# Small-head attentions: value jobs of a group in two pairs, with the turning of the next maxima behind the second pair

## What is computed

```python
# L2: causal
Q = relu(queries @ Wq + bq); K = relu(keys @ Wk + bk); V = relu(values @ Wv + bv)   # 16 heads, d = 16
scores = where(key_masks == 0, NEG, Q_ @ K_^T / d**0.5); scores = where(tril == 0, NEG, scores)
out = softmax(scores) @ V_;  out = relu(out @ Wo + bo);  x = normalise(queries + out)
# L3: banded self attention, then full cross attention, then the feed-forward part
mask = (j <= i) & (i - j < 64); bias = slopes[:, None, None] * (j - i)
x = layernorm(x + mha(x, x, ..., mask, bias)); x = layernorm(x + mha(x, mem, ..., None, None))
x = layernorm(x + gelu(x @ w1 + b1) @ w2 + b2)
```

## Time and profile before

| what | value |
|---|---|
| median of three runs | 1582.44 us |
| lowest, highest | 1578.88, 1588.16 us |
| the profiled execution, its own time | 1586.47 us |
| its span, first to last instruction | 1584.7 us |
| mean granted TensorE clock | 0.978 |
| TensorE busy | 1434.6 us, 91% of the span |
| VectorE busy | 864.1 us, 55% |
| ScalarE busy | 716.6 us, 45% |

### The profile page before, as it was taken

How to read it: one execution, slowest core, us unless ns; L and a number is a source line. 1 busy time by engine, 2 the same in 40 slices (tenths; PEclk the granted TensorE clock), 3 DMA queues, 4 the chain that set the end, 5 groups by cost and what they waited for, 6 DMA issues and landing times.

```text
span 1584.7 us, 24180 instructions
## 1 busy us (share of the span) xinstructions
PE 1434.6 (91%) x8296; PEld 710.5 (45%) x8328; DVE 864.1 (55%) x2099; ACT 716.6 (45%) x1177; POOL 263.5 (17%) x138
## 2 busy tenths in 40 slices
PE   5999998888999989888999998989899999989886
PEld 2336554433533654542443464553263355455334
DVE  2663565585266266567346536557635634655762
ACT  0663353355266234427446525353725632725462
POOL 1004131301100413220110223121011030303001
PEclk9999999999999999999999999999999999999998
DMA  9000405303200230530310032242031005043210
GB/s 341 21 1 12 103 1 94 69 13 114 68 1 7 36 72 2 101 73 1 126 55 1 8 57 51 41 88 47 5 123 55 1 8 99 10 69 66 40 61 13
DMA packets 44776, 85.28 MB, mean 54 GB/s; under 512 B 10464, under 2 KB 27872, under 8 KB 44384
## 3 DMA queue, kind: packets, MB, share of 16 engines
q1 hardware_dynamic: 41136, 73.17, 18.5%
q10 hardware_dynamic: 3504, 10.39, 3.3%
HBM read 43.68 MB, written 2.10 MB: 29 GB/s over the span
## 4 chain that ended last, share of the span: by engine, by line
PE 62%; DVE 16%; issue 10%; ACT 6%; DMA 3%; SPq 2%; ACTq 1%; POOL 0%; DVEq 0%; POOLq 0%
PE ring L1286 8%; PE obank L1296 8%; PE ring L1276 7%; DVE nmax L1075 7%; PE ring L1252 6%; PE ring L1463 6%; PE ring L1352 4%; PE ring L1605 3%; PE obank L1513 3%; ACT q_all L771 3%; PE ring L1201 3%; PE ring L1454 2%; DMA q_all<-q_parts 2%; SPq L413 2%; DVE rbuf L1094 2%
## 5 line engine op out<-in xcount | busy, mean ns | idle before, releaser
L1075 DVE TENSOR_REDUCE nmax<-ring 128x2 f32<-128x1024 f32 (+1 forms) x192 | 217.8, 1174 | 41.1 <-PE ring L1463 32.2
L679 ACT ACTIVATE region_e<-region_d,nmin 128x512 f32<-128x512 f32 x256 | 182.7, 714 | 84.6 <-DVE nmin L936 83.3
L936 DVE CUSTOM_DVE_ANT_0 region_d<-ring,maskb 128x512 f32<-128x512 f32 x256 | 165.9, 685 | 97.6 <-issue 95.4
L784 ACT ACTIVATE region_e<-ring 128x1024 f32<-128x1024 f32 x192 | 183.0, 992 | 48.9 <-PE ring L1463 29.7
L771 ACT ACTIVATE q_all<-ring 2x1024 fp32r<-2x1024 bf16 x96 | 97.6, 1016 | 210.1 <-PE ring L1524 209.5
L606 POOL TENSOR_TENSOR nat_x<-nat_n,rows 128x1024 f32<-128x1024 f32 x16 | 37.7, 2355 | 605.5 <-DVE nat_n L985 459.2
L1286 PE MATMUL ring<-region_q 64*128 64x512 f32 x512 | 128.5, 621 | 7.0 <-ACT region_q L668 5.4
L1071 DVE TENSOR_REDUCE nmax<-ring 128x4 f32<-128x512 f32 (+1 forms) x96 | 86.1, 910 | 78.3 <-PE ring L1454 77.7
L1296 PE MATMUL obank<-region_e,vs 128*64 128x512 f32 x512 | 124.0, 605 | 0.0
L1454 PE MATMUL ring<-cbf 64*128 64x128 bf16 (+2 forms) x1280 | 122.9, 270 | 0.0
L780 ACT ACTIVATE region_e<-ring 128x768 f32<-128x768 f32 (+1 forms) x96 | 74.1, 776 | 47.6 <-PE ring L1454 47.0
(11 more groups left out here) (193 smaller groups left out, 2155.2 us busy)
## 6 DMA issues: line engine op xcount, KB each, us to landing
q_all<-q_parts SPq DMA_DIRECT2D x192, 64.0 KB, 2.4
region_e<-in_w_f SPq DMA_DIRECT2D x8, 1024.0 KB, 5.7
k_tiles_a<-k_parts SPq DMA_DIRECT2D x96, 64.0 KB, 2.3
k_tiles_b<-k_parts SPq DMA_DIRECT2D x96, 64.0 KB, 2.3
q_all<-q_parts ACTq DMA_DIRECT2D x96, 64.0 KB, 3.2
wvo<-in_wv SPq DMA_DIRECT2D x5, 1024.0 KB, 5.1
wqk<-in_wq SPq DMA_DIRECT2D x4, 1024.0 KB, 8.6
wqk<-in_wk SPq DMA_DIRECT2D x4, 1024.0 KB, 10.9
```

Of the source, the lines that this page charges most:

```text
L679: ins = act.activation(e0[:, n % E0, h, :], sm0[:, n % 2, h, :], ACT.Exp, bias=nmin0[:, n, h:h + 1], scale=-1.0, accum_out=sum0[:, n, h:h ...
L784: act.activation(e16[:, n % 4, 2 * u:2 * u + 2, 0:nq], slot((a, "B", g, kt, u))[:, :, 0:nq], ACT.Exp)\
L936: ins = dve.tensor_tensor_reduce(out=sm0[:, n % 2, h, :], in0=slot(("S0", p, kt))[:, h, :], in1=maskb[:, :], scale=-1.0, scalar=3.0e38, op ...
L1075: dve.tensor_reduce(nmax[:, qt, 2 * u:2 * u + 2], slot(name)[:, :, 0:nk], AX.X, ALU.max, negate=True)\
```

## The change

Nothing is added and no job is dropped. V(g-1, 2) no longer stands by itself ahead of V(g-1, 3): both now come where V(g-1, 3) stood. V(g, 1), which stood behind T(g+1) and an A job, now comes directly behind V(g, 0), ahead of T(g+1). The order of A, B and T jobs among themselves stays, and with it `JOBS` and the slots; ScalarE and VectorE see the same list as before, since they skip V. The end of the last group stays as well.

```diff
@@ group_steps
-            if g and i in ((0, 2) if a == BANDED else (0, 1)):
-                steps.append(("V", g - 1, 3 if i else 2))
+            if g and i == (2 if a == BANDED else 1):
+                steps += [("V", g - 1, 2), ("V", g - 1, 3)]
...
         if i == NT:
-            steps.append(("V", g, 0))
-            steps += [("T", g + 1)] if g + 1 < GROUPS else []
+            steps += [("V", g, 0), ("V", g, 1)] + ([("T", g + 1)] if g + 1 < GROUPS else [])
         steps += ahead(a, g + 2, i - NT)
-        if i == NT:
-            steps.append(("V", g, 1))
```

## The result

The changed kernel takes 1618.15 us (median of 4 runs, 1617.02 to 1620.81) against 1585.3 for the kernel before (1578.88 to 1590.25, 4 runs, one more than stood ahead of the prediction). The ratio is 1.0204, 95% interval 1.0172 to 1.0236: 32.9 us slower. The forecast was 18.7 us slower, 1601.0 with a range up to 1614. The direction was right, the size was not; the time lies in the band of the rival "the clock falls more often", 1607 to 1619.

A forecast was written before the change was run, and what follows sets the result against it. The prediction took a loop of engines (T, copies, A, maxima, `mcol`) as the bound; CAUSAL 2.37, BANDED -0.12 and FULL 2.42 make 4.67 us a pass, 18.7 in four passes: 1601 us, range 1591 to 1614.

The forecast's parts named there:

- the clock falls more often: Rival: idle time behind each T and A220 lowers TensorE's clock, 6 to 18 us on top, 1607 to 1619; chance 0.15.
- The loop: Small-head attentions: T releases copies, then A, VectorE's maxima, `mcol`, next T; delaying T delays all; 4.67 us a pass.
- the terms of V01 ahead of T: CAUSAL: the pair's second value job delays T1 and T2 by 0.64 us each and T3 by 0.31.
- The 0.32 that a second job of 192 columns was estimated to add: BANDED and FULL: estimated cost in us of the second value job of a pair, against 0.46 for one alone.
- V02 in CAUSAL: CAUSAL groups 1 and 2: V02 moved back to V03 delays B110 and `mcol` by 0.44 us each; bounds 0 and 0.68.
- FULL's first group: FULL, V01 ahead of T1, starting at half clock: +0.96 us, bounds 0.64 and 1.61.
- FULL's last group: FULL's end: nothing saved, since the last V jobs wait for the exponentials there.
- CAUSAL's last group: CAUSAL's end, no A jobs left to delay: TensorE saves 0.10 us of up to 0.35.
- the 0.21 from a mask's start to V02's: TensorE: 0.21 us read from the trace, taken as agreeing with a drain at changes of tiling mode.
- TensorE is the bound: Rival: fewer changes of tiling win, 0.25 us for each of 72 value places, 18 us faster, 1564; chance 0.08.
- Nearly cancelled: Rival: other releases catch CAUSAL's terms and last groups give back 0.35, 7.6 us left, 1585 to 1593; chance 0.12.
- The check named for this: Signs: granted clock's mean below 0.97 means the clock has its share; FULL's V00 to V10 grows from 14.01 to about 15.4.

The follow-up runs named there:

- the first half of the change: Only V01 moved ahead of T, V02 and V03 left in place, against the kernel before: 1625.91 us, ratio 1.0259.
- the filling: Five useless matmuls behind T: changed kernel, FULL alone 1607.51 us, all three attentions 1610.54 us; only V01 ahead of T, all three attentions 1600.34 us.
- The run of V02 alone: Only V02 moved back to V03, V01 left behind T and the next A job, against the kernel before: 1601.26 us, ratio 1.0099.
- The run without FULL: CAUSAL and BANDED as changed, FULL as before, against the kernel before: 1596.03 us, ratio 1.0048.

## Why the prediction was right, and where it was wrong

*The loop held.* "What delays T delays these jobs by as much": in CAUSAL the terms of V01 ahead of T were 0.64, 0.64 and 0.31, and the first half of the change showed just these. In FULL, at full clock, T1 to T2 grew by 0.73 and T2 to T3 by 0.73 to 0.74 (forecast 0.41 + 0.32 each). BANDED moved by 0, +0.15, -0.09 and -0.34 (0, 0.25, -0.02, -0.35). The 0.32 that a second job of 192 columns was estimated to add could have been read: the pair of the earlier trace rows is not the only one before, BANDED's V30 and V31 are another and cost 0.79 (677.78 to 678.57), 0.33 more than the 0.46 of one.

*Terms that were mis-sized, slightly.* V02 in CAUSAL: 0.31 in each of two groups, on top of the first half (10.82 to 11.13), where 0.44 was taken. FULL's first group: T0 to T1 is 12.29 with the filling against 10.97 before, +1.32, where 0.96 was taken, inside the bounds 0.64 and 1.61. Up to T2 this evens out: 26.31 against 24.67, +1.64, where 0.96 + 0.41 + 0.32 = 1.69 was taken. T0 to T1 holds a slow stretch before and after, so that this term is not the loop's alone. FULL's last group: +0.31 (14.74 to 15.05) where nothing was taken. With -0.14 in CAUSAL's last group a pass comes to 2.08 - 0.28 + (1.64 + 0.73 + 0.31) = 4.48 us, or 17.9 in four, against 4.67 and 18.7. The line through the runs gives 17.3. The sum of the prediction was right for what it summed, in part because small errors cancel. One reading was loose without harm: of the 0.21 from a mask's start to V02's, 0.10 is what a mask costs ahead of a score job too (588.57 to 588.67), so 0.11 is left for the change of tile.

*The step that failed* is the one that put the clock's rival aside: "in this trace T2 of FULL lasts 0.62 against T1's 1.03, thus ran at full clock in spite of the waits around it, which speaks against". The waits around T2 before were 0.47 and 0.28, with V11 between them; the change makes them one of 1.47 without V11. That T2 was at full clock next to short waits said nothing about a long one. Nor could T itself have told: after the change T1, T2 and T3 of FULL last 0.62 too (733.01, 747.97, 764.12 in the second pass), and the granted clock falls to 0.50 some 5 to 6 us behind each of them. So the sum had nothing for further slow stretches, and the runs put about 14 to 16 us there. The prediction had named the idle time (0.78 and 0.68), its place (behind each T and A220), and even a price (6 to 18 us), and gave it 0.15. The filled runs show that the idle time behind T is a cause: matmuls that compute nothing of use gave back 10.6 us of the whole change and 25.6 of its first half. The run of V02 alone, 10.8 of its 15.7 us at the clock by the line, points to V02's idle place as another, which no run filled. The run without FULL shows that FULL's part of the change pays most of it.

By the Trainium skill, "TensorE: Matmul & The Clock Gate", Part 1, the low clock is the default, and activity lifts it. The prediction cited this and let one row outweigh it; here the runs side with the page: the mean clock is 0.964 with the idle time and 0.973 with part of it filled.

*The other rivals fell.* "TensorE is the bound" wanted 1564; line 768's waits grew by 33.8 us instead. "Nearly cancelled" wanted 1585 to 1593; with the whole change no other release caught CAUSAL's terms (with V02 alone its second term was caught, 0.02 of 0.44).

*The check named for this held:* the mean clock at 0.964, below 0.97, and V00 to V10 in FULL at 15.96 (730.15 to 746.11), where 15.4 was forecast without a slow clock in the second group and 14.01 measured before.

*Open.* Why the waits of 1.12 in CAUSAL and BANDED leave the clock nearly alone when FULL is as before, yet BANDED's last group slows in three passes when V01 stands ahead of T everywhere; why V01 alone costs more than the whole change, all of it at the clock (0.960 against 0.9655, at the same height above the line); and how much of FULL's loss is V02's idle place, which wasn't filled. The 7.2 us that the rest of the kernel gave back are slow stretches that did not come at the openings; the code there is the same, and two other runs with the same code there lack them as well. What decides in which execution they come is not known.

## What to carry to other kernels

Before a job is moved out of a wait, add up the idle time that it leaves in one piece, on an engine whose granted clock already shows 0.50 somewhere in that stage, and price a slow stretch there as a term of the sum, not as a remote rival. Ahead of a job that a loop of engines waits for, a filler costs its full pitch, however well it pairs with its neighbour. To tell a lost clock from a lost dependency, fill the idle place with work of no use and see that the distances at full clock stay: what comes back was the clock. Filling a wait that had always been there gained nothing here.

## What the runs showed of the hardware

The times of one and the same program spread over 18 us (1576.4 to 1594.9), and 0.7 us is left of that spread when the mean granted clock is taken out. A wait of 1.36 us at a pass's opening is followed by a granted clock of 0.50 in one trace and by 1.00 in another. Filling such a place in the kernel before gained nothing in the median (1.0012 and 0.9992). In the executions that were profiled the stretch left the filled place and others stood elsewhere: in FULL's second group (T1 to T2 14.68 in two passes of four, 13.3 in the others), or in FULL when the openings were filled (14.9 against 13.7).
